# Gathered rows of experts two to eight: loaded in 32 by 32 squares and turned on VectorE, in place of turns on TensorE

## The chip, the core and the metric

The kernel runs on one core of a Trainium2 chip. The core has a matrix engine (TensorE, PE), a vector engine (VectorE, DVE), an activation engine (ScalarE, ACT), a general engine (GpSimd, POOL) and a queue engine (SyncE, SP) that issues transfers; sixteen DMA engines move data between the chip's memory and the on-chip memory of 128 partitions. Each engine works through its own list of instructions in the order written, and they wait for each other by semaphores. The metric is the device time of one execution in microseconds.

## What is computed

A block of a transformer over 16 sequences of 256 tokens with 256 features: cross attention with 16 heads, then a mixture of eight experts of which each token uses two. An expert has room for 640 tokens. All in float32. Cut to what matters here:

```python
x = x + xattn(layernorm(x), ctx)
x_flat = layernorm(x).reshape(4096, 256)
gates = softmax(x_flat @ router_w + router_b)
# per expert: its tokens in order of position, at most 640
buf = zeros((8, 641, 256)).at[expert, slot].add(dispatched)[:, :640]
h = gelu(einsum('ecd,edh->ech', buf, w1) + b1)      # 256 -> 1024
out = einsum('ech,ehd->ecd', h, w2) + b2            # 1024 -> 256
y = einsum('ned,ne->nd', out[expert, slot], gates)
x = x + y
```

## The kernel before

**The table.** While attention runs, GpSimd scatters each token's row into `slot_table` in the chip's memory: 8 x 640 slots, a row of 265 floats (1060 bytes). Columns 0 to 255 are the token's features, column 256 (`ID`) its number, 257 to 264 its gates. The experts gather nothing: expert e reads the 640 rows e x 640 and on.

**Two factors for one.** Every product is taken as three of a reduced float type: a high part (`bufh`, `w1h`, `hidh`), cut on ScalarE or VectorE, and the rest (`bufl`, `w1l`, `hidl`), which VectorE gets by subtraction (`rest_of`, L1072).

Experts are numbered from 0, as in the code: the title's second to eighth are experts 1 to 7.

**An expert.** `up` (L842) has eight chunks j of 128 hidden columns, each with 2 halves of 320 tokens x 2 chunks of features x 3 products = 12 matmuls at L615. ScalarE takes gelu of chunk j (L1044) into one of two `hid` buffers; VectorE splits it into `hidh` (cast, L1328) and `hidl` (L1072) (`split_hid`). `hid` is double buffered, so gelu j waits until chunk j-2 is split, and `up` j waits for gelu j-2. `down` (L862) has five steps of 128 tokens with 8 x 3 = 24 matmuls at L875; in its first step it waits for hidden chunk after hidden chunk. VectorE adds the bias and multiplies with the gate (`weigh`, L1337 and L1338), and GpSimd adds the 128 rows of `y` to the output by an indirect transfer (L591).

**The other factor.** The matmuls of `up` need the tokens' rows with features on the partitions, while a load brings tokens on the partitions. For expert 0 the gather is done by matmuls from the last steps of attention. For experts 1 to 7 `turn_rows` (three calls per expert, of 2, 2 and 1 tiles of 128 tokens) exists on three engines: TensorE turns 128 by 128 tiles through the identity into PSUM (L838), ScalarE copies them to `bufh`, VectorE takes the rest to `bufl`. The calls for expert e+1 stand in `up` of expert e behind chunks 3, 5 and 7 (`TURN_AFTER`); those for expert 1 stand in `down` of expert 0. `up` of an expert waits for its `buf_lo`.

**The loads.** SP issues, for each expert, the rows (`load_rows`, into one of two `rows` buffers, after the y of the expert before the last are written) and behind them both weights (`load_w`, L390 and L391), which all go through one queue in this order. Weights of the next expert are split while `down` runs (`split_w`), pieces alternating with `weigh` on VectorE.

Of the kernel before, what the change touches and what calls it, by code (L numbers as in the profile page):

```python
# [27 lines left out]
P = 128  # L28
B, S, D = 16, 256, 256
# [5 lines left out]
DC = D // P  # L35
NE, HID = 8, 1024
# [14 lines left out]
TURNS = -(-ET // 2)  # L51
TURN_AFTER = (3, 5, 7)
# [125 lines left out]
def build(nc, x, ctxt, wq, wk, wv, wo, bo, rw, rb, w1, b1, w2, b2, out):  # L178
    es = ExitStack()
    with es:  # L180
# [88 lines left out]
        rows = sb(late, "rows", [2, ET, ROW])  # L269
# [56 lines left out]
        def _(sp):  # L326
# [66 lines left out]
            def load_rows(e):  # L393
                if e == 0:
                    sp.dma_start(rows[:, 0, :, D:ROW], table[0:CAP, D:ROW].rearrange("(s p) w -> p s w", p=P))\
                      .then_inc(sem("rows_first"), 16)
                    return
                if e >= 2:
                    sp.wait_ge(sem("y"), ET * (e - 1))
                sp.dma_start(rows[:, e % 2, :, :],  # L400
                             table[e * CAP:(e + 1) * CAP, :].rearrange("(s p) w -> p s w", p=P))\
                  .then_inc(sem(f"rows_in{e % 2}"), 16)
# [195 lines left out]
        def _(pe):  # L598
# [231 lines left out]
            def turn_rows(e, u):  # L830

                rows_ready(pe, e)
                at = TURNS * (e - 1) + u
                pe.wait_ge(sem("buf_lo"), max(2, at + 1))
                for s in range(2 * u, min(2 * u + 2, ET)):
                    for kk in range(DC):
                        col = (s - 2 * u) * D + kk * P
                        mm = pe.transpose(psum[:, at % 2, col:col + P],  # L838
                                          rows[:, e % 2, s, kk * P:(kk + 1) * P], ident[:, :])
                mm.then_inc(sem("turn_rows"), 1)  # L840

            def up(e):  # L842
                r = e % 2
                pe.wait_ge(sem("buf_lo"), 2 + TURNS * e if e else 1)
                pe.wait_ge(sem("wsplit_lo"), WSPLITS * e + WSPLITS // 2)
                for j in range(HC):
# [12 lines left out]
                    if 1 <= e < NE - 1 and j in TURN_AFTER:  # L859
                        turn_rows(e + 1, TURN_AFTER.index(j))  # L860

            def down(e):  # L862
                r = e % 2
                pe.wait_ge(sem("wsplit_lo"), WSPLITS * (e + 1))
                for s in range(ET):
# [12 lines left out]
                    if e == 0 and s < TURNS:  # L878
                        turn_rows(1, s)
# [7 lines left out]
        def _(act):  # L887
# [136 lines left out]
            def turn_rows(e, u):  # L1024
                at, s0, s1 = TURNS * (e - 1) + u, 2 * u, min(2 * u + 2, ET)
                act.wait_ge(sem("turn_rows"), at + 1)
                if e >= 2:
                    act.wait_ge(sem("up"), HC * (e - 1))
                src = psum[:, at % 2, :].rearrange("p (s k c) -> p k s c", k=DC, c=P)
                for kk in range(DC):  # L1030
# [357 lines left out]
```

## Time and profile before

| what | us |
|---|---|
| median of three runs | 1008.44 (1007.81 to 1008.87) |
| the profiled execution, its own time | 1009.7 |
| its span, first to last instruction | 1008.0 |
| TensorE busy | 969.1 (96%) |
| VectorE busy | 780.9 (77%) |
| ScalarE busy | 624.3 (62%) |
| GpSimd busy | 288.5 (29%) |

Attention takes the span up to about 750 us, the eight experts the rest. A busy TensorE isn't TensorE at its peak, since matmuls overlap in the profile; the chain of work that ended last shows how many microseconds a group of them takes of the time. The granted TensorE clock was at its full 1.00 (2.4 GHz) in the stretches of the experts that are read below. A DMA share of 1 means sixteen DMA engines busy; a short window may show more, since a transfer counts where it starts.

### The profile page before, as it was taken

The page shows a single profiled execution, that of the slowest core. Times are in us where ns is not written, and L with a number is a line of the kernel's source. Part 1 is how long each engine was busy: PE and PEld are TensorE (multiplying, and loading weights), DVE is VectorE, ACT ScalarE, POOL GpSimd, SP SyncE. Part 2 cuts the span into 40 slices and gives each one's busy share as a digit, 9 for nine tenths or more (in the row PEclk, how much of TensorE's full clock was granted, in tenths as well). Part 3 has the DMA queues.
Part 4 walks back from the last instruction along what each step waited for, and adds up shares of the span by engine and source line. Part 5 has one row for each costly group of instructions (what it writes and reads, how often), then busy time and mean ns, then how long its engine had stood idle before and what let it go on. Part 6 is the DMA issues. An engine that isn't in the chain of part 4 may idle for free. (4 is left out here: it accounts for less than half of the span.)

```text
span 1008.0 us, 23338 instructions
## 1 busy us (share of the span) xinstructions
PE 969.1 (96%) x8434; PEld 876.0 (87%) x8434; DVE 780.9 (77%) x2093; ACT 624.3 (62%) x1739; POOL 288.5 (29%) x442
## 2 busy tenths in 40 slices
PE   7889999999999999999999999999978999999996
PEld 6778888888888888888888888888768999999995
DVE  6897778878887878878797888877867766777662
ACT  5777776777677767776777677776724333344330
POOL 4542021314132231314123231302253333222233
PEclk9999999999999999999999999999989999999998
DMA  8440101001010101101010101000214543444522
GB/s 240 140 122 2 33 2 33 26 30 54 3 52 15 33 13 33 44 2 44 11 33 6 33 9 33 17 1 16 95 44 154 137 118 75 99 131 127 137 28 27
DMA packets 49057, 56.77 MB, mean 56 GB/s; under 512 B 5948, under 2 KB 44842, under 8 KB 48816
## 3 DMA queue, kind: packets, MB, share of 16 engines
q1 hardware_dynamic: 40112, 46.30, 14.8%
q0 software_dynamic: 8832, 8.98, 5.6%
q8 instruction: 69, 1.13, 0.5%
q14 instruction: 44, 0.36, 0.1%
HBM read 36.01 MB, written 24.20 MB: 60 GB/s over the span
## 5 line engine op out<-in xcount | busy, mean ns | idle before, releaser
L938 ACT ACTIVATE prob<-psum,negmax 128x256 f32<-128x256 f32 x512 | 240.0, 487 | 90.6 <-DVE negmax L1124 89.6
L888 ACT ACTIVATE probt<-psum 128x512 f32<-128x512 f32 x256 | 157.3, 623 | 53.5 <-PE psum L698 52.5
L1124 DVE TENSOR_REDUCE negmax<-psum 128x2 f32<-128x512 f32 x256 | 160.1, 683 | 24.8 <-PE psum L682 24.7
L1135 DVE TENSOR_SCALAR prob<-prob,invtot 128x256 f32<-128x256 f32 x512 | 164.2, 384 | 4.5
L698 PE MATMUL psum<-ident,prob 128*128 128x128 f32 x1024 | 150.5, 273 | 2.4 <-DVE prob L1135 1.6
L1044 ACT ACTIVATE hid<-psum,b1t 128x640 f32<-128x640 f32 x64 | 50.8, 796 | 129.1 <-PE psum L615 124.2
L698 PEld LDWEIGHTS psum<-ident,prob 128*128 128x128 f32 x1024 | 119.7, 140 | 11.7 <-ACT probt L888 2.1
L712 PE MATMUL psum<-probt,v 128*64 128x256 f32 x1024 | 124.6, 385 | 0.0
L550 POOL DMA_INDIRECT slot_table<-row,picki x64 | 66.9, 1045 | 174.6 <-DVE picki L1281 147.5
L591 POOL DMA_INDIRECT out_rows<-y,rowi x40 | 66.8, 1671 | 162.1 <-DVE y L1338 155.1
L938 ACT ACTIVATION_READ_ACCUMULATOR prob<-psum,negmax 128x1 f32 x512 | 112.2, 219 | 0.0
L712 PEld LDWEIGHTS psum<-probt,v 128*64 128x64 f32 x1024 | 67.8, 136 | 36.3 <-issue 0.3
L875 PE MATMUL psum<-w2h,hidh 128*128 128x256 f32 x320 | 92.2, 288 | 1.3 <-DVE hidl L1072 1.3
L485 POOL TENSOR_SCALAR shifted<-ln_mean_var 128x2 f32<-128x2 f32 x32 | 7.3, 229 | 298.7 <-issue 256.4
L875 PE MATMUL psum<-w2l,hidh 128*128 128x256 f32 x320 | 91.0, 285 | 0.0
L875 PE MATMUL psum<-w2h,hidl 128*128 128x256 f32 x320 | 91.0, 284 | 0.0
L682 PE MATMUL psum<-kh,qh 64*128 64x256 f32 x512 | 80.8, 304 | 4.7 <-ACT prob L938 1.7
L615 PE MATMUL psum<-bufh,w1h 128*128 128x320 f32 x256 | 80.4, 314 | 1.4 <-DVE bufl L1072 0.9
L729 PE MATMUL psum<-woh,ah 128*128 128x256 f32 x256 | 75.2, 294 | 6.6 <-DVE kl L1072 5.7
L615 PE MATMUL psum<-xth,wqh 128*128 128x256 f32 x256 | 79.0, 308 | 0.5 <-DVE xtl L1072 0.5
L615 PE MATMUL psum<-bufh,w1l 128*128 128x320 f32 x256 | 79.1, 309 | 0.0
L615 PE MATMUL psum<-bufl,w1h 128*128 128x320 f32 x256 | 79.1, 309 | 0.0
(192 smaller groups left out, 2744.7 us busy)
## 6 DMA issues: line engine op xcount, KB each, us to landing
w1r<-in_w SPq DMA_DIRECT2D x8, 1024.0 KB, 8.2
w2r<-in_w SPq DMA_DIRECT2D x8, 1024.0 KB, 10.4
slot_table<-blank SPq DMA_DIRECT2D x8, 662.5 KB, 9.8
rows<-slot_table SPq DMA_DIRECT2D x7, 662.5 KB, 5.4
xin<-in_x SPq DMA_DIRECT2D x16, 256.0 KB, 2.9
out_rows<-x SPq DMA_DIRECT2D x16, 256.0 KB, 3.2
c<-in_ctxt SPq DMA_DIRECT2D x16, 128.0 KB, 3.1
c<-in_ctxt SPq DMA_DIRECT2D x32, 64.0 KB, 2.8
```

The costliest lines, as they stand in the source:

```text
L550: pool.indirect_dma_start(out=table, out_offset=bass.IndirectOffsetOnAxis(ap=picki[:, b % 3, k, t:t + 1], axis=0), in_=row[:, b % 3, t, :] ...
L591: pool.indirect_dma_start(out=out_rows, out_offset=bass.IndirectOffsetOnAxis(ap=rowi[:, e % 2, s:s + 1], axis=0), in_=y[:, e % 2, s, :], i ...
L615: mm = pe.matmul(dst, lhs, rhs, start=(j == 0), stop=(j == len(terms) - 1))
L682: mm = pe.matmul(psum[:, 2 * cc + h, qb * S:(qb + 1) * S], a[r, m % 2, cc, cols], w[r, m % 2, cc, :], start=(j == 0), stop=(j == len(terms ...
L698: mm = pe.transpose(psum[:, TURN_BANK[u], kb * S + qb * P:kb * S + (qb + 1) * P], prob[:, m % 2, u, qb, kb * P:(kb + 1) * P], ident[:, :])
L712: mm = pe.matmul(dst[h * HD:(h + 1) * HD, cc * S:(cc + 1) * S], v[:, b % 2, kb, cols], probt[:, m % 2, 2 * cc + h, kb, :], start=(kb == 0) ...
L729: mm = pe.matmul(dst[:, 0:D], a[:, b % 2, c, tt], w[:, c, :], start=(c == 0 and j == 0), stop=(c == PAIRS - 1 and j == 2))
L875: mm = pe.matmul(dst, a[:, j, ss], w[:, j, :], start=(j == 0 and m == 0), stop=(j == HC - 1 and m == 2))
L888: copy = lambda dst, src, **kw: act.activation(dst, src, ACT.Copy, **kw)
L938: last = act.activation(prob[:, m % 2, u, qb, :], psum[:, u, qb * S:(qb + 1) * S], ACT.Exp, bias=negmax[:, m % 2, u, qb:qb + 1], accum_out ...
L1124: dve.tensor_reduce(negmax[:, m % 2, u, :], psum[:, u, :].rearrange("p (q s) -> p q s", q=ST), AX.X, ALU.max, negate=True).then_inc(sem("m ...
L1135: last = dve.tensor_scalar(prob[:, m % 2, u, qb, :], prob[:, m % 2, u, qb, :], invtot[:, m % 2, u, qb:qb + 1], None, ALU.mult)
```

## The change

The table, its scatter, and the matmuls of `up` and `down` stay. What changes is how the rows of experts 1 to 7 become `bufh` and `bufl`:

- **Loads.** `rows` keeps only the 9 columns of number and gates. The 256 feature columns come into a new tile `blocks` by eight loads per expert. The load for feature chunk k and group g of 32 features puts, on partition g x 32 + i, row c x 32 + i for all c from 0 to 19, 32 floats of each: squares of 32 tokens by 32 features. Each of these loads is 32 x 20 runs of 128 bytes. They wait for `turned` of the expert before.
- **Turns.** VectorE transposes each 32 by 32 square in place (`square_rows`): one instruction of 128 x 640 for each feature chunk, from `blocks` to `turned`.
- **Splits.** ScalarE copies `turned` to `bufh` (`head_rows`) and VectorE subtracts (`rest_rows`), 128 x 640 each, two per expert in place of six.
- **Places.** In `up` of expert e: the turns behind the split of chunks 1 and 2, heads behind gelu 3 and 4, rests behind chunks 5 and 6. For expert 1 they stand in `down` of expert 0. TensorE has no part in it any more.

```diff
-TURNS = -(-ET // 2)
-TURN_AFTER = (3, 5, 7)
+SQ = 32
+GROUPS = P // SQ
+SQUARE_AFTER = (1, 2)
+HEAD_AFTER = (3, 4)
+REST_AFTER = (5, 6)
...
-        rows = sb(late, "rows", [2, ET, ROW])
+        blocks = sb(late, "blocks", [DC, CAP // SQ, SQ])
+        turned = sb(late, "turned", [DC, CAP])
+        rows = sb(late, "rows", [2, ET, ROW - D])
...
                 if e >= 2:
                     sp.wait_ge(sem("y"), ET * (e - 1))
                 sp.dma_start(rows[:, e % 2, :, :],
-                             table[e * CAP:(e + 1) * CAP, :].rearrange("(s p) w -> p s w", p=P))\
-                  .then_inc(sem(f"rows_in{e % 2}"), 16)
+                             table[e * CAP:(e + 1) * CAP, D:ROW].rearrange("(s p) w -> p s w", p=P))\
+                  .then_inc(sem(done), 16)
+                if e == 0:
+                    return
+                if e >= 2:
+                    sp.wait_ge(sem("turned"), DC * (e - 1))
+                squares = table[e * CAP:(e + 1) * CAP, 0:D].rearrange("(c i) (k g j) -> k g i c j", i=SQ, k=DC, g=GROUPS)
+                for k in range(DC):
+                    for g in range(GROUPS):
+                        sp.dma_start(blocks[g * SQ:(g + 1) * SQ, k, :, :], squares[k, g])\
+                          .then_inc(sem(f"blocks_in{k}"), 16)
...
-                pe.wait_ge(sem("buf_lo"), 2 + TURNS * e if e else 1)
+                pe.wait_ge(sem("buf_lo"), 2 + DC * e if e else 1)
...
-                    if 1 <= e < NE - 1 and j in TURN_AFTER:
-                        turn_rows(e + 1, TURN_AFTER.index(j))
...
-            def turn_rows(e, u):
...
+            def head_rows(e, k):
+                act.wait_ge(sem("turned"), DC * (e - 1) + k + 1)
                 if e >= 2:
                     act.wait_ge(sem("up"), HC * (e - 1))
...
+                copy(bufh[:, e % 2, k, :], turned[:, k, :]).then_inc(sem("buf_hi"), 1)
...
                     for piece in range(WSPLITS):
                         split_w(e + 1, piece)
-                        if e == 0 and piece < TURNS:
-                            turn_rows(1, piece)
+                        if e == 0 and 1 <= piece <= DC:
+                            head_rows(1, piece - 1)
...
+            def square_rows(e, k):
+
+                dve.wait_ge(sem(f"blocks_in{k}"), 16 * GROUPS * e)
+                if e >= 2:
+                    dve.wait_ge(sem("buf_lo"), 2 + DC * (e - 1))
+                dve.transpose(turned[:, k, :], blocks[:, k, :, :].rearrange("p c j -> p (c j)"))\
+                   .then_inc(sem("turned"), 1)
+
+            def rest_rows(e, k):
+                dve.wait_ge(sem("buf_hi"), 2 + DC * (e - 1) + k + 1)
+                rest_of(bufl[:, e % 2, k, :], turned[:, k, :], bufh[:, e % 2, k, :]).then_inc(sem("buf_lo"), 1)
...
                     weigh(e, s)
-                    if e == 0 and s < TURNS:
-                        turn_rows(1, s)
+                    if e == 0 and s == 1:
+                        for k in range(DC):
+                            square_rows(1, k)
+                    if e == 0 and 2 <= s < 2 + DC:
+                        rest_rows(1, s - 2)
```

SP's queue around the loads for one expert, before: rows, then the two weights.

```order
L400 DMA rows<-slot_table 128x5x265
L390 DMA w1r<-in_w 128x2x1024
L391 DMA w2r<-in_w 128x8x256
L400 DMA rows<-slot_table 128x5x265
L390 DMA w1r<-in_w 128x2x1024
```

And after (the line numbers are those of the changed kernel):

```order
L404 DMA rows<-slot_table 128x5x9
L414 DMA blocks<-slot_table 32x20x32 x8
L395 DMA w1r<-in_w 128x2x1024
L396 DMA w2r<-in_w 128x8x256
L404 DMA rows<-slot_table 128x5x9
```

Eight loads stand between the small rows and the weights.

VectorE's order in `up` of an expert, before (a cast and a subtraction per chunk, pairs of rests between):

```order
L1328 CAST hidh<-hid 128x640
L1072 TENSOR_TENSOR hidl<-hid,hidh 128x640
L1072 TENSOR_TENSOR bufl<-psum,bufh 128x256 x2
L1328 CAST hidh<-hid 128x640
L1072 TENSOR_TENSOR hidl<-hid,hidh 128x640
L1328 CAST hidh<-hid 128x640
L1072 TENSOR_TENSOR hidl<-hid,hidh 128x640
L1072 TENSOR_TENSOR bufl<-psum,bufh 128x256 x2
```

This piece runs from chunk 3 to the second pair of rests, behind chunk 5; the third stands behind chunk 7. After, the same engine from chunk 1 on:

```order
L1323 CAST hidh<-hid 128x640
L1064 TENSOR_TENSOR hidl<-hid,hidh 128x640
L1305 STREAM_TRANSPOSE turned<-blocks 128x640
L1323 CAST hidh<-hid 128x640
L1064 TENSOR_TENSOR hidl<-hid,hidh 128x640
L1305 STREAM_TRANSPOSE turned<-blocks 128x640
L1323 CAST hidh<-hid 128x640
L1064 TENSOR_TENSOR hidl<-hid,hidh 128x640
```

and from chunk 5 on:

```order
L1323 CAST hidh<-hid 128x640
L1064 TENSOR_TENSOR hidl<-hid,hidh 128x640
L1064 TENSOR_TENSOR bufl<-turned,bufh 128x640
L1323 CAST hidh<-hid 128x640
L1064 TENSOR_TENSOR hidl<-hid,hidh 128x640
L1064 TENSOR_TENSOR bufl<-turned,bufh 128x640
L1323 CAST hidh<-hid 128x640
L1064 TENSOR_TENSOR hidl<-hid,hidh 128x640
```

Both turns and both rests now stand ahead of the split of chunk 7, the last piece above.

## Rows read from the trace of the kernel before

**Rows 1.** The page, part 1: busy time, share and instructions of each engine.

```profile
PE 969.1 (96%) x8434; PEld 876.0 (87%) x8434; DVE 780.9 (77%) x2093; ACT 624.3 (62%) x1739; POOL 288.5 (29%) x442
```

**Rows 2.** The chain that ended last, experts 0 to 3: start us, us, what.

```profile
792.09 7.04 PE psum L615 x48
...
851.23 7.05 PE psum L615 x48
858.28 0.44 PE psum L838 x4
858.72 3.52 PE psum L615 x24
...
866.21 0.22 PE psum L838 x2
866.42 14.40 PE psum L875 x120
```

**Rows 3.** Timeline of TensorE, expert 3: start us, us, instruction.

```profile
851.07 0.31 PE L615 MATMUL psum<-bufh,w1h 128*128 128x320 f32 x1
```

**Rows 4.** Timeline of VectorE, experts 0 and 3; in brackets the idle time before.

```profile
774.68 0.49 DVE L1328 CAST hidh<-hid 128x640 fp32r<-128x640 f32 x1
...
775.94 0.49 DVE L1328 CAST hidh<-hid 128x640 fp32r<-128x640 f32 x1
...
853.86 0.50 DVE L1328 CAST hidh<-hid 128x640 fp32r<-128x640 f32 x1 [1.78 <-issue]
...
860.42 0.75 DVE L1072 TENSOR_TENSOR bufl<-psum,bufh 128x256 fp32r<-128x256 f32 x2
...
867.60 0.82 DVE L1072 TENSOR_TENSOR hidl<-hid,hidh 128x640 fp32r<-128x640 f32 x1
868.34 0.48 DVE L1072 TENSOR_TENSOR bufl<-psum,bufh 128x128 fp32r<-128x128 f32 x2
```

**Rows 5.** Timeline of ScalarE, the first two gelus of expert 3.

```profile
853.03 0.80 ACT L1044 ACTIVATE hid<-psum,b1t 128x640 f32<-128x640 f32 x1 [11.45 <-PE psum L615]
854.79 0.80 ACT L1044 ACTIVATE hid<-psum,b1t 128x640 f32<-128x640 f32 x1 [0.96 <-PE psum L615]
```

**Rows 6.** Timeline of SP's issues, experts 3 and 4.

```profile
852.11 0.37 SPq L400 DMA_DIRECT2D rows<-slot_table  x1
...
881.70 0.37 SPq L400 DMA_DIRECT2D rows<-slot_table  x1
882.16 0.47 SPq L390 DMA_DIRECT2D w1r<-in_w  x1
882.68 0.47 SPq L391 DMA_DIRECT2D w2r<-in_w  x1
```

**Rows 7.** Landing of the rows of expert 0 (L395); busy time, clock, DMA share, GB/s.

```profile
DMA to landing us min/median/max: 2.0/2.0/2.0
...
767.80:768.00 0.20, 0.20 (x3) 0.20 (x2) 0.20 (x1) 0.20 (x1) 0.20 (x1) 1.00 0.86 46
772.00:773.00 1.00, 1.00 (x9) 1.00 (x8) 0.97 (x2) 0.00 (x0) 0.29 (x1) 1.00 1.05 372
```

**Rows 8.** Last scatter of expert 2 on GpSimd's timeline; windows around the one before.

```profile
852.87 1.57 POOL L591 DMA_INDIRECT out_rows<-y,rowi  x1 [1.34 <-DVE y L1338]
...
852.00:853.25 1.25, 1.25 (x10) 1.25 (x9) 0.08 (x1) 0.22 (x1) 0.38 (x1) 1.00 0.96 105
853.25:853.50 0.25, 0.25 (x4) 0.25 (x3) 0.00 (x0) 0.25 (x1) 0.25 (x1) 1.00 0.12 17
```

**Rows 9.** Weights of expert 1: SP's issue, ScalarE's and VectorE's first piece.

```profile
772.37 0.37 SPq L390 DMA_DIRECT2D w1r<-in_w  x1
...
777.93 1.06 ACT L888 ACTIVATE w1h<-w1r 128x1024 fp32r<-128x1024 f32 x1 [2.28 <-DMA w1r<-in_w]
...
779.10 1.23 DVE L1072 TENSOR_TENSOR w1l<-w1r,w1h 128x1024 fp32r<-128x1024 f32 x1 [1.72 <-ACT w1h L888]
```

**Rows 10.** The page, part 6: KB each, median us from issue to landing.

```profile
w1r<-in_w SPq DMA_DIRECT2D x8, 1024.0 KB, 8.2
```

More of the change, by code:

```diff
@@ L393, in load_rows @@
             def load_rows(e):
[L394 to L397, printed above, removed]
+                done = "rows_first" if e == 0 else f"rows_in{e % 2}"
                 if e >= 2:
@@ L1022, in gathered @@
                 last.then_inc(sem("buf_hi"), 1)
-            def turn_rows(e, u):
-                at, s0, s1 = TURNS * (e - 1) + u, 2 * u, min(2 * u + 2, ET)
-                act.wait_ge(sem("turn_rows"), at + 1)
+            def head_rows(e, k):
+                act.wait_ge(sem("turned"), DC * (e - 1) + k + 1)
                 if e >= 2:
                     act.wait_ge(sem("up"), HC * (e - 1))
-                src = psum[:, at % 2, :].rearrange("p (s k c) -> p k s c", k=DC, c=P)
-                for kk in range(DC):
-                    last = copy(bufh[:, e % 2, kk, s0 * P:s1 * P].rearrange("p (s c) -> p s c", c=P),
-                                src[:, kk, 0:s1 - s0, :])
-                last.then_inc(sem("buf_hi"), 1)
+                copy(bufh[:, e % 2, k, :], turned[:, k, :]).then_inc(sem("buf_hi"), 1)
             for half in range(2):
@@ L1046, in _ @@
                                    bias=b1t[:, e, j:j + 1]).then_inc(sem("gelu"), 1)
-                    if 1 <= e < NE - 1 and j in TURN_AFTER:
-                        turn_rows(e + 1, TURN_AFTER.index(j))
+                    if 1 <= e < NE - 1 and j in HEAD_AFTER:
+                        head_rows(e + 1, HEAD_AFTER.index(j))
                 if e + 1 < NE:
@@ L1306, in gathered @@
                 last.then_inc(sem("buf_lo"), 1)
-            def turn_rows(e, u):
-                at, s0, s1 = TURNS * (e - 1) + u, 2 * u, min(2 * u + 2, ET)
-                dve.wait_ge(sem("buf_hi"), 2 + at + 1)
-                src = psum[:, at % 2, :].rearrange("p (s k c) -> p k s c", k=DC, c=P)
-                for kk in range(DC):
-                    part = lambda a: a[:, e % 2, kk, s0 * P:s1 * P].rearrange("p (s c) -> p s c", c=P)
-                    last = rest_of(part(bufl), src[:, kk, 0:s1 - s0, :], part(bufh))
-                last.then_inc(sem("buf_lo"), 1)
+            def square_rows(e, k):
[7 more added lines that the diff above has]
+                rest_of(bufl[:, e % 2, k, :], turned[:, k, :], bufh[:, e % 2, k, :]).then_inc(sem("buf_lo"), 1)
             def row_numbers(e):
@@ L1320, in row_numbers @@
                     dve.wait_ge(sem("added"), 16 * ET * (e - 1))
-                dve.tensor_copy(rowi[:, e % 2, :], rows[:, e % 2, :, ID]).then_inc(sem("rowi"), 1)
+                dve.tensor_copy(rowi[:, e % 2, :], rows[:, e % 2, :, ID - D]).then_inc(sem("rowi"), 1)
             def split_hid(at):
@@ L1346, in _ @@
                     split_hid(HC * e + j)
-                    if 1 <= e < NE - 1 and j in TURN_AFTER:
-                        turn_rows(e + 1, TURN_AFTER.index(j))
+                    if 1 <= e < NE - 1 and j in SQUARE_AFTER:
+                        square_rows(e + 1, SQUARE_AFTER.index(j))
+                    if 1 <= e < NE - 1 and j in REST_AFTER:
+                        rest_rows(e + 1, REST_AFTER.index(j))
                 row_numbers(e)
```

13 lines of the change are left out of this document (1 added, 12 removed).

## The prediction

> **What bounds the kernel now.** I read the page first: TensorE is busy for 969.1 of 1008.0 us, VectorE for 780.9 [rows 1]. All that the change touches lies in the last quarter, the eight experts. There the chain that ended last is TensorE alone. For expert 3 it reads 7.05 us (four chunks of `up`), 0.44 for four turns, 3.52, 0.44 and 3.52 again, 0.22 for two turns, and 14.40 of `down`: 29.6 us in all and no gap [rows 2]. So an expert costs what TensorE needs, and anything taken off it is a gain until another engine is late. Who would be late is read from the timelines of the same expert. I count from the start of its `up`, 851.07 [rows 3]. A chunk of `up` takes 1.76 us; gelu j ends, and the split of hidden chunk j can begin, at 2.79 + 1.76 j (853.86 for j = 0) [rows 4, 5].
>
> **What TensorE loses.** Ten turns of 128 by 128 per expert take 0.44 + 0.44 + 0.22 = 1.10 us of the chain [rows 2]; 70 in all, 7.7 us for seven experts. This is the most that can be won, 0.8%.
>
> **What VectorE gets.** A split of a hidden chunk holds the engine for 1.27 us when nothing keeps it waiting: cast at 774.68, next cast at 775.94; the subtraction of 640 columns holds it for 0.74 (867.60, next start 868.34) [rows 4]. Before, the rests in `up` were two pairs of 256 and one of 128, 0.75 us for a pair, of which one pair came after chunk 7 [rows 4]. Now there are two turns of 640 columns, after chunks 1 and 2, and two rests of 640, after chunks 5 and 6: all four come ahead of chunk 7. A rest of 640 is the same form as the hidden subtraction, 0.74. A turn by VectorE is not in the trace. Its nearest rows are the cast of 640 (0.49) and that subtraction (0.83 busy, 0.74 held); I take 0.75, since it also passes 640 columns of 4 bytes one by one, and keep 0.5 and 1.5, twice it, as bounds.
>
> Walked through, with the squares always there: chunk 1 is done at 4.55 + 1.27 = 5.82; turn 0 to 6.57; chunk 2 to 7.84; turn 1 to 8.59; chunks 3 and 4 to 11.13; then 0.46 us idle, since gelu 5 allows 11.59; chunk 5 to 12.86; rest 0.74; chunk 6 to 14.88; rest; chunk 7 begins at 15.63 where gelu would have allowed 15.11, and its subtraction ends at 16.98. TensorE now reaches `down` at 14.08 and needs hidden chunk 7 for the 22nd matmul, 21 x 0.12 = 2.52 later (14.40 us over 120 matmuls [rows 2]), at 16.60. Before it had 0.5 us to spare: 866.42 + 2.52 = 868.94 against 867.60 + 0.82 [rows 2, 4]. So there is a stall of 0.4 to 0.45 us per expert that no late transfer causes. The gain is then 0.65 us for each of the six experts turned for within an `up`, not 1.10.
>
> **The squares, on which it hangs.** SP may load the rows of the next expert once the last y of the previous one is written: rows at 852.11, 1.04 after the start, then both weights [rows 6]. Now SP issues the small rows (9 columns), eight square loads, and only then the weights. An issue costs about 0.5 us (881.70, 882.16, 882.68) [rows 6], so the squares are issued at 1.5, 2.0, ... 5.0. A load of 640 runs of 36 bytes landed 2.0 us after its issue [rows 7]; by issue alone the fourth square lands at 5.0 and the eighth at 7.0. VectorE asks for them at 5.82 and 7.84. Because of the 0.46 us idle after chunk 4 they may come at 6.28 and 8.30; every us after that is a us of VectorE, of chunk 7, and so of TensorE. TensorE notices it late, but in full.
>
> Will the transfers keep up with the issues? Each square load is 640 runs of 128 bytes, 320 a DMA engine for all eight. Prices of a run: for 36 bytes, 46 GB/s at a share of 0.86 is 0.86 x 16 x 36 / 46 = 10.8 ns; for the 1060 bytes of a whole row, 372 GB/s at 1.05 is 48 ns [rows 7]. On the line between, 128 bytes cost 10.8 + 92/1024 x 37 = 14 ns. Bounds: 11 (no more than the short one) and 25 (half of the long one). At 14, 320 runs are 4.5 us. They start when the engines have dealt with the scattered rows of y that are still there until 853.25 (share 0.96 up to it, 0.12 behind it [rows 8]), and with the small rows, 640 of which held the engines some 0.65 us at 36 bytes each: at about 2.95. A landing follows its last run by some 0.35. So squares of k = 1 are there at 2.95 + 4.5 + 0.35 = 7.8, in time. But the last scatter of y of the previous expert is issued at 852.87, 1.8 after the start [rows 8], in the midst of them. One such scatter keeps all engines busy for 1.1 us (1.25 us at 0.96 [rows 8]). Before, it competed with rows and weights that nobody awaited for 10 us; now it may stand between the runs of k = 1. With it they land at 8.9. I take this: the lateness is 8.9 - 8.30 = 0.6, the stall 0.45 + 0.6 = 1.05 us, and six experts together gain 6 x 0.05 = 0.3 us.
>
> The Trainium skill ("DMA: Bandwidth & Descriptors", section Why small descriptors are slow) speaks against such loads: a packet costs about 3 cycles beside one for each 32 bytes. As an estimate by that page, 128 bytes cost 7/5 of 36 bytes, 15 ns where the line above gives 14, and the time would be some 2 us longer; no run of the kernel before shows packets of 128 bytes.
>
> **Expert 1, turned for in `down` of expert 0.** Here the squares (issued from about 768) take 4.5 us of the DMA engines where the old rows took 640 x 48 ns / 16 = 1.9, ahead of the weights that are issued at 772.37; ScalarE already waited 2.28 us for these weights, until 777.93, and VectorE 1.72 for ScalarE [rows 9]. They come some 2 us later. In VectorE's order now stand: weight split, y, weight split, y, both turns, weight split, y, rest, weight split, y, rest, y; from 781.1 the second rest ends near 792.7, because the third weight split has to wait for ScalarE, which waits for the first turn before it goes on. `up` of expert 1 waits for that rest; it began at 792.09 before [rows 2]. So the 1.10 us are not won here, and 0.6 is lost (between 1.1 won and 1.5 lost).
>
> **What is hidden.** The weights of the next expert come about 4.5 us later than before (8.2 us after an issue at 1.5 gives 9.7 [rows 10], now near 14); ScalarE wants them after gelu 7, at 15.1, the second half at 17. That just holds; if the squares take 3 us more, it still costs nothing, since the stall then moves gelu 7 too. ScalarE has two copies of 640 instead of six small ones, in an engine that idles 0.96 us before each gelu [rows 5]. Wherever it would stall without this cover, the price is that of the lateness itself.
>
> **The sum.** Profiled execution 1009.7 us (span 1008.0, 1.7 around it), 1.3 above the median 1008.44. Change: -7.7 (turns) + 1.1 (expert 1 keeps nothing of it) + 0.6 (expert 1 late) + 6 x 1.05 (stalls) = +0.3. So 1010.0 for the profiled one and 1008.7, say 1009, for the median.
>
> **The rivals.**
> A, faster: the scatter does not meet the squares, or it does so only behind them, and 128 bytes cost no more than 14 ns. Then the stall is 0.45: -6 x 0.65 + 0.6 = -3.3, 1005.1. If VectorE's turn also costs 0.5 us, the stall is nearly gone: down to 1001. For it: issue and landing alone leave 1.3 us to spare at k = 1. Against it: the scatter's place at 1.8.
> C, slower: the runs are dearer than the line between two prices says, because they are short, start anywhere (a row of the table is 1060 bytes) and fill 32 partitions only. At 20 ns, k = 1 lands at 2.95 + 6.4 + 0.35 + 1.1 = 10.8, the stall is 2.95, the change 6 x 1.85 + 0.6 = +11.7: 1020. At 25 ns 1030. Slower by over 2 us begins at 15 ns with the scatter in between, at 18 without.
> D, slower: a turn on VectorE costs 1.5 us. With forecast landings it adds about 0.75 behind k = 1: +5, 1014.
> E, far slower: the loads are not moved in runs of 128 bytes but in single words. Then 10,240 packets an engine at 10.8 ns are 110 us an expert, against 29.6: beyond 1500 us. The Trainium skill ("VectorE: DVE Perf Modes", The three transpose paths) calls a plain copy that transposes by its strides 19 times slower than the crossbar. Speaking against it: the inner 32 columns stay contiguous on both sides, and the built program has them as 32x20x32.
>
> **How the numbers follow.** The forecast, landing near 8.9 with its own range 1005 to 1013, has 0.40; A (1001 to 1006) 0.30; C (1013 to 1030) 0.24; D 0.05; E 0.01. A measurement of this kernel tells 0.2%, 2 us, from no change. Of the forecast's 0.40 I give 0.05 to faster, 0.24 to the same, 0.11 to slower. So faster 0.35, same 0.24, slower 0.41. The range 1002 to 1023 leaves out the ends of A and C, and E.
>
> **What would show it.** No row of TensorE with `rows`; ten turns gone. In `up`, VectorE's turn near 0.83 us busy, its idle time before the second turn put down to a DMA, 1.1 us or less; the load of `blocks` landing 2.5 to 4 us after issue; TensorE's idle time in `down` before the 22nd matmul, put down to `hidl`, about 1.0 us in each of six experts. An expert's period of 29.5 us would bear the forecast out, 28.9 A, over 30.5 C. I am wrong in kind if TensorE waits for `bufl` or for the weights of experts 2 to 7, or not at all.

## The result, and the profile after

| | before | after |
|---|---|---|
| median, us | 1008.58 (1007.51 to 1009.22, 6 runs) | 1015.06 (1014.34 to 1016.82, 6 runs) |
| ratio | | 1.0068 (95% interval 1.0055 to 1.0081) |
| profiled execution, own time | 1009.7 | 1014.72 |
| its span | 1008.0 | 1012.9 |

The changed kernel is slower by 6.5 us, more than the 2 us that a measurement can tell. The two profiled executions stand 5.0 us apart, because that of before lies above its median and that of after below its own. What follows explains the 4.9 us between the spans; for the rest there are no traces, only a lead at the end of this section.

The page of after, part 1 (answers to [rows 1]):

```profile
PE 966.0 (95%) x8364; PEld 870.5 (86%) x8364; DVE 789.3 (78%) x2079; ACT 621.7 (61%) x1711; POOL 286.7 (28%) x442
```

TensorE has 70 instructions fewer, as the change says, and is busy 3 us less; yet the span is longer. So the question is where TensorE now stands still. The waits of TensorE in the experts (engine, line, waited for: us in total, times, longest):

```profile
PE psum L874 <- DVE hidl L1064: 7.5, 8, 1.1
PE psum L874 <- DVE y L1333: 3.2, 2, 2.6
PE psum L628 <- ACT hid L1036: 0.9, 2, 0.5
PE psum L628 <- DVE bufl L1064: 0.5, 1, 0.5
```

Mostly `down` waits for a hidden chunk (`hidl`), as forecast. Two of these eight waits, 0.64 us each, lie in `down` of expert 0 and are in the kernel before too; the other six, one in each of experts 1 to 6, are new (6.2 us). The two waits for `y` and the one for `bufl` are in expert 0, below. TensorE's timeline at that place in expert 3, whose `up` starts at 855.29 (throughout I take 1.96 us before gelu 0, as 851.07 stands to 853.03 before):

```profile
871.77 0.28 PE L874 MATMUL psum<-w2h,hidl 128*128 128x256 f32 x1
873.09 0.39 PE L874 MATMUL psum<-w2h,hidh 128*128 128x256 f32 x1 [1.04 <-DVE hidl L1064]
```

The idle time in the brackets is less than the stall: matmuls of `down` otherwise start 0.12 us apart, and these two start 1.32 apart, 1.20 later than they could, of which the profile counts only what lies behind the modelled end of the first.

And the chain that ended last, from the last square load of that expert to `down` (start us, us, what), where [rows 2] showed TensorE alone:

```profile
860.10 0.51 SPq L414
...
860.65 3.75 DMA blocks<-slot_table
...
864.43 0.85 DVE turned L1305
...
869.03 0.73 DVE bufl L1064
...
871.03 0.73 DVE bufl L1064
...
872.21 0.84 DVE hidl L1064
...
873.09 10.94 PE psum L874 x89
```

It reads: the eighth issue, 3.75 us until it lands, VectorE from the second turn through five splits and two rests without a pause, and then TensorE. VectorE's timeline (answers to [rows 4]) shows that both turns wait, not only the second:

```profile
861.85 0.84 DVE L1305 STREAM_TRANSPOSE turned<-blocks 128x640 f32<-128x640 f32 x1 [0.66 <-DMA blocks<-slot_table]
862.62 0.45 DVE L1323 CAST hidh<-hid 128x640 fp32r<-128x640 f32 x1
...
864.43 0.85 DVE L1305 STREAM_TRANSPOSE turned<-blocks 128x640 f32<-128x640 f32 x1 [0.50 <-DMA blocks<-slot_table]
865.20 0.45 DVE L1323 CAST hidh<-hid 128x640 fp32r<-128x640 f32 x1
```

A turn holds VectorE for 0.77 us (861.85 to 862.62). In the numbers below "turn 0/turn 1" is the start of the two turns after the start of `up`, and the period is from one `up` to the next. An expert without turns would take 28.49 us: the 29.58 us of [rows 2]'s kind less 1.10, and experiment D shows it six times.

| expert in whose `up` the turns stand | 1 | 2 | 3 | 4 | 5 | 6 |
|---|---|---|---|---|---|---|
| turn 0 | 8.19 | 6.78 | 6.56 | 6.83 | 6.70 | 6.57 |
| turn 1 | 10.35 | 9.36 | 9.14 | 9.41 | 8.92 | 9.14 |
| period | 30.98 | 30.01 | 29.78 | 30.05 | 29.56 | 29.77 |
| stall (period - 28.49) | 2.49 | 1.52 | 1.29 | 1.56 | 1.07 | 1.28 |

The 4.9 us are: +2.7 in these six periods (180.15 against 6 x 29.58), +1.83 in expert 0 (34.63 us from its gelu 0 to that of expert 1, before 32.80), and some +0.45 that begins ahead of the experts (gelu 0 of expert 0 is at 761.63 instead of 761.09) and is partly made good in the last. This last part isn't the change's: in the twelve profiles of this document, all with the same attention, that gelu stands anywhere from 760.04 to 762.79.

Expert 0's part starts in SP's queue (answers to [rows 6] and [rows 9]), then ScalarE's and VectorE's first weight pieces, and expert 1's first gelu:

```profile
768.58 6.90 SPq L414 DMA_DIRECT2D blocks<-slot_table  x8
775.59 0.45 SPq L395 DMA_DIRECT2D w1r<-in_w  x1
```

```profile
780.79 2.00 ACT L885 ACTIVATE w1h<-w1r 128x1024 fp32r<-128x1024 f32 x2 [4.60 <-DMA w1r<-in_w]
...
796.26 0.80 ACT L1036 ACTIVATE hid<-psum,b1t 128x640 f32<-128x640 f32 x1 [6.12 <-PE psum L628]
```

```profile
781.95 1.23 DVE L1064 TENSOR_TENSOR w1l<-w1r,w1h 128x1024 fp32r<-128x1024 f32 x1 [4.04 <-ACT w1h L885]
```

The weights of expert 1 are issued at 775.59 instead of 772.37. ScalarE waits 4.60 us for them instead of 2.28, VectorE 4.04 instead of 1.72. VectorE does the first y of expert 0 behind that split, and TensorE has to stop for it, 2.6 us, since `down` has two halves of PSUM for its steps.

The 32.80 us that this is compared with hold something else. I wrote of the kernel before that TensorE's clock was full in all the stretches read. It wasn't: in `down` of expert 0 its profile has 3.4 us at the lower of the two levels (1.2 GHz, granted share 0.50), which begin just after TensorE had waited twice for a hidden chunk. The kernel after has none there. The windows of before, then of after:

```profile
777.40:780.80 3.40, 3.40 (x16) 3.40 (x17) 1.67 (x3) 2.66 (x4) 0.00 (x0) 0.50 0.72 241
```

```profile
777.80:781.20 3.40, 3.31 (x27) 3.29 (x27) 0.11 (x2) 0.41 (x1) 0.00 (x0) 1.00 1.02 392
```

From 777.35 on, with 99 matmuls and all ten turns to go, TensorE took 14.74 us until 792.09, where 99 x 0.12 + 1.10 = 12.98 would do: about 1.7 us go to the clock. At full clock before, expert 0 is about 3.5 us dearer after the change, not 1.83, and the spans would stand 6.6 us apart, which is what the medians show (6.5). That the unprofiled executions of the kernel before lack this stretch is likely by that, but not shown. Expert 0 also differs by itself: in eight of the changed kernels (after, A, B, D, F, G, H, M) TensorE, VectorE and ScalarE have the same work in it, and it takes from 34.54 to 35.86 us.

### The profile page after: what moved, and what is told of

Same layout as the page of the kernel before. It is cut to its first block and busy times, and to the rows that moved or that the text cites. A ratio compares the mean times of both kernels' runs of the same rounds, so it can differ in the third digit from the quotient of the medians.

```text
span 1012.9 us, 23197 instructions
## 1 busy us (share of the span) xinstructions
PE 966.0 (95%) x8364; PEld 870.5 (86%) x8364; DVE 789.3 (78%) x2079; ACT 621.7 (61%) x1711; POOL 286.7 (28%) x442
```

## The experiments

My theory after the result: the stall is the sum of two causes, VectorE's order (both rests ahead of chunk 7) and the late arrival of the squares; the arrival is late because the runs of 128 bytes need the DMA engines longer than forecast, with a scatter among them; and expert 0 pays for weights queued behind squares. Rivals: the arrival is set by SP's issues (eight at 0.55 us), or the scatter alone makes it late, or the order on VectorE matters little. Each run below stands beside runs of the kernel before on the same chip; its ratio is to those. In the kernel after, the ratio was 1.0068.

### A. The rests behind chunk 7

```diff
-                    if 1 <= e < NE - 1 and j in REST_AFTER:
-                        rest_rows(e + 1, REST_AFTER.index(j))
+                    if 1 <= e < NE - 1 and j == HC - 1:
+                        for k in range(DC):
+                            rest_rows(e + 1, k)
```

> The changed kernel with one move: the two rests of 128x640 on VectorE stand behind the split of hidden chunk 7 instead of behind chunks 5 and 6. Theory (VectorE's chain from the second turn to chunk 7 is too long, and TensorE waits for chunk 7 in the first step of down): the chain gets 1.48 us shorter, the waits for chunk 7 in experts 2 to 6 (1.1 to 1.6 us) all but go, that of expert 1 (2.5) falls to about 1, some 8 us in all: 1007. Rival (only the arrival of the squares counts, and VectorE has room behind it): no change, 1015.

Measured: 1010.0 us (1008.44 to 1012.25, 10 runs), ratio 1.0008 (0.9998 to 1.0017). That is between the 1007 of the theory and the 1015 of its rival: about 0.6% comes back for two rests, 1.48 us of VectorE, that no longer stand ahead of chunk 7. The turns wait as before (6.68 and 9.32 in expert 3), and the periods are 30.90, 29.41, 28.79, 29.14, 28.66, 28.67. With turn 1 at 9.15 and 9.20 (experts 5 and 6) only 0.17 is left of the stall, as much as M below has with no late square at all; with 11.45 and 9.94 (experts 1 and 2) there is more, 2.2 and 0.7. So lateness up to about 9.2 is absorbed, and what is beyond it is paid in full. It is paid at another place than forecast: TensorE no longer waits for a hidden chunk in `down` of these experts, but in `up` for gelus (0.90 and 0.82 us in expert 1), which wait for late splits. The gain was larger than the order's own 0.45 x 6, because it also swallows lateness.

### B. Only the squares of k = 0 are loaded, experts 2 to 7

```diff
-                for k in range(DC):
+                for k in range(DC if e == 1 else 1):
...
-                dve.transpose(turned[:, k, :], blocks[:, k, :, :].rearrange("p c j -> p (c j)"))\
+                dve.transpose(turned[:, k, :], blocks[:, k if e == 1 else 0, :, :].rearrange("p c j -> p (c j)"))\
```

> The changed kernel, but for experts 2 to 7 only the four square loads of feature chunk 0 are made, and both turns read them; the half of the rows with features 128 to 255 is left out, so the output is not the reference's. VectorE's work and order are unchanged. Theory (the late arrival of the second four loads adds to the stall): turn 1 no longer waits, the stall falls from 1.1 to 1.6 us to 0.5 to 0.7 in experts 2 to 6 and by more in expert 1: about 5 us less, 1010. Rival (VectorE's longer order alone makes the stall): 1015. Rival (the loads cost nothing but their issue on SP): the same 1010 with the turn's wait gone, so this one does not tell issue from transfer.

Measured: 1014.72 us (1012.51 to 1015.36, 4 runs), ratio 1.0057 (1.0041 to 1.0074). A miss, and the most useful one: half the bytes and half the issues (2.18 us in place of 4.90) bring almost nothing (the profiled execution, 1012.51, is the lowest of the four). Turn 1 reads what the loads of k = 0 brought and has no wait of its own. VectorE's timeline, expert 3 of this kernel, whose `up` starts at 853.28:

```profile
860.10 0.84 DVE L1306 STREAM_TRANSPOSE turned<-blocks 128x640 f32<-128x640 f32 x1 [0.92 <-DMA blocks<-slot_table]
```

Turn 0 is at 6.82, as late as in the kernel after (6.56). Turn 1 then follows it directly, 2.0 later, at 8.82. My sum had put the scatter behind the squares of k = 0 and let turn 0 be in time; it is turn 0 that the scatter meets first. Periods were 30.41, 29.35, 29.46, 30.36, 29.63, 29.35; in expert 4, where turn 0 is at 7.72, the period is longer than with the full load (30.05).

### C. The weights of expert 1 ahead of its squares

```diff
-            load_rows(1)
+            load_rows(1, (0,))
             load_w(1)
+            load_rows(1, (1,))
```

(Part 0 of `load_rows` is the small rows, part 1 the squares.)

> The changed kernel, but for expert 1 SP issues both weights ahead of the eight square loads. Theory (in down of expert 0, 1.8 us are lost because the weights of expert 1 are issued at 775.6 instead of 772.4 and come 3 us later): ScalarE has w1r near 777.9 again; the squares then come near 784, about when VectorE asks for them; up of expert 1 starts 1 to 2 us earlier, 1013.5. Rival (the loss there comes from VectorE's and ScalarE's new order of turns, heads and rests): no change, 1015.

Measured: 1015.37 us (1014.53 to 1017.35, 4 runs), ratio 1.0068 (1.0049 to 1.0087). No change in the time, yet expert 0 has its 1.1 us: 33.56 from gelu 0 to gelu 0 instead of 34.63 and below all eight profiles named above; ScalarE waits 1.8 us for w1 instead of 4.6. The six periods took it back: 181.57 against 180.15, with turn 1 anywhere from 8.81 to 10.39. This run showed that arrival differs by over 0.5 us from expert to expert and from kernel to kernel though nothing near those loads was changed, and that one repair can't be read from the total while the other stall stands.

### D. All row work of experts 2 to 7 in `down` of the expert before

```diff
-                    if 1 <= e < NE - 1 and j in SQUARE_AFTER:
-                        square_rows(e + 1, SQUARE_AFTER.index(j))
-                    if 1 <= e < NE - 1 and j in REST_AFTER:
-                        rest_rows(e + 1, REST_AFTER.index(j))
...
+                    if 1 <= e < NE - 1 and 1 <= s < 1 + DC:
+                        square_rows(e + 1, s - 1)
+                    if 1 <= e < NE - 1 and s == 3:
+                        for k in range(DC):
+                            rest_rows(e + 1, k)
```

The heads go behind the weight splits on ScalarE.

> The changed kernel with all row work of experts 2 to 7 moved from up to down of the expert before: turns behind the y of steps 1 and 2, both rests behind that of step 3, the heads behind the weight splits. The loads stay. Theory: down leaves VectorE some 6 us idle, the squares are there 8 us before they are asked for, TensorE waits for nothing: period 28.5 us for six experts, -9.3 us: 1006. Rival (the loads of 128-byte runs themselves hold up weights, scatters or the split of hidden chunks): periods stay above 29, 1009 or more.

Measured: 1005.57 us (1004.89 to 1006.00, 6 runs), ratio 0.9963 (0.9951 to 0.9976): faster than before. The chain from `up` of expert 2 on:

```profile
822.84 14.08 PE psum L628 x96
836.92 14.41 PE psum L874 x120
851.33 14.08 PE psum L628 x96
865.41 14.41 PE psum L874 x120
```

TensorE alone, 28.49 us an expert six times over; the turns wait for nothing at 20.8 and 23.7. This is [rows 2] without its turns, and the 1.10 us of the forecast's first term is all there: 29.58 - 28.49 = 1.09.

### F. The fifth scatter of experts 0 to 6 left out

```diff
-                for s in range(ET):
+                for s in range(ET if e == NE - 1 else ET - 1):
```

(and the counts that wait for it; the fifth tile of y is not added for these experts.)

> The changed kernel without the scatter of the fifth tile of y (tokens 512 to 639) of experts 0 to 6, which is left out, so those rows of the output lack a part. It is issued 1.8 us after up starts, amid the square loads. Theory (it holds the DMA engines for about 1 us while the squares of chunk 0, or of chunk 1, are on their way, and makes the first turn start at 6.6 to 6.8 us and the second at 9.1 to 9.4 after the start of up): turn 0 at 6.0, turn 1 at 8.3, the stall per expert 1.3 -> 0.5, expert 1 gains 1 more: 1015 -> 1009. Rival (runs of 128 bytes are slow by themselves, or their start is what is late): turns where they are, 1015.

Measured: 1011.63 us (1010.84 to 1013.24, 5 runs), ratio 1.0030 (1.0017 to 1.0044). Turn 0 comes in time in experts 2, 3, 5 and 6 (5.92, 5.82, 5.87, 5.90), where it came at 6.56 to 6.78. So the scatter is what made turn 0 late in these. In expert 4 it is at 6.80 all the same; SP's eight issues took 5.38 us there instead of 4.38. But turn 1 hardly gains: 8.50, 8.92, 9.57, 9.04, 8.66 in experts 2 to 6, a mean of 8.94 against 9.19. I had expected 8.3. The windows of this kernel in expert 3, `up` from 852.80, tell why (window, its length, busy us and count of PE, PEld, DVE, ACT, POOL, clock, DMA share, GB/s):

```profile
855.75:860.80 5.05, 5.05 (x37) 5.05 (x36) 4.44 (x7) 2.35 (x4) 0.00 (x0) 1.00 0.88 134
...
855.80:856.80 1.00, 1.00 (x9) 1.00 (x8) 0.97 (x2) 0.28 (x1) 0.00 (x0) 1.00 0.73 105
...
859.80:860.30 0.50, 0.50 (x6) 0.50 (x5) 0.47 (x2) 0.26 (x1) 0.00 (x0) 1.00 0.42 66
```

The busy time is 5.05 x 0.88 = 4.44 us for 320 runs an engine, 13.9 ns for one. (The bytes in the window are some 3% more than the squares', so this is a little high; the trace's own packets of 128 bytes there take 13.7 ns on average.) But they are not packed: at the beginning the share is 0.73, near the end 0.42, and the second turn starts at 861.72, 8.92 after `up`. By these packets the stream begins 2.75 us after `up` and its last one ends at 8.35, so it is 5.6 us long; the landing follows 0.54 later.

### G. Each square load with half its runs, experts 2 to 7

```diff
-                        sp.dma_start(blocks[g * SQ:(g + 1) * SQ, k, :, :], squares[k, g])\
+                        c = CAP // SQ if e == 1 else CAP // SQ // 2
+                        sp.dma_start(blocks[g * SQ:(g + 1) * SQ, k, 0:c, :], squares[k, g][:, 0:c, :])\
```

> The changed kernel; for experts 2 to 7 each of the eight square loads brings only rows 0 to 319 (10 squares of 20 for each group; the rest of the tile keeps what it had), so the output is not the reference's. Same eight issues on SP, half the runs. Theory (transfer of the runs, 0.7 to 0.9 us per load, sets the arrival, not the issue at 0.55): turn 0 at 6.0 or earlier, turn 1 no longer waits for a DMA (8.0 or earlier), 5 to 6 us less: 1009. Rival (SP's issues set it): turns stay where they are, 1015. Rival (the scatter in between holds them whatever their number): turn 0 stays at 6.6 or later, turn 1 is better, 1013.

Measured: 1009.92 us (1008.49 to 1011.67, 10 runs), ratio 1.0012 (1.0003 to 1.0021). Eight issues as before (4.15 to 4.17 us in most experts), half the runs, and over 5 us come back. Turn 1 follows turn 0 by 2.0 in all six; three of the periods are 28.96 or 28.97. So it isn't SP's pace that makes turn 1 late, but the runs in the transfers. They act on SP as well: in the kernel after, one or two of the eight issues took about 1 us in each of experts 2 to 6, and the eighth went out at 5.4 to 6.2 after `up`; here it went out at 5.1 to 5.2 (expert 4: 6.2). How much of the lateness goes through these held-up issues, and how much through the engines alone, no run separates. Turn 0 still comes at 5.90 to 7.30.

### H. The squares issued as soon as their tile is free, 20 us earlier

```diff
-            load_rows(2)
+            load_rows(2, (1,))
+            load_rows(2, (0,))
...
-                    load_rows(e + 1)
+                    load_rows(e + 1, (1,))
+                    load_rows(e + 1, (0,))
```

(Part 1 is the squares again; they no longer wait for y, only for `turned`, and the small rows stay where they were.) All computing stays where it was. The squares are issued 8.7 us after the start of the `up` before, and the weights no longer stand behind them.

> The changed kernel, all instructions of the compute engines in their places; SP issues the squares of an expert as soon as the tile is free again, before it waits for y: some 20 us before they are turned, while the small rows stay where they are. Theory (two terms make the stall, the squares' arrival and VectorE's order): the arrival is gone, the order remains: split of chunk 7 ends 0.52 us later than in an expert without row work, period 28.49 + 0.52 = 29.0 in all six experts (now 29.6 to 31.0), 6 us less: 1009. Rival (arrival alone): period 28.5, 1006. Rival (order alone): 1015.

Measured: 1008.08 us (1006.76 to 1009.74, 10 runs), ratio 0.9998 (0.9989 to 1.0008). VectorE's timeline, expert 3 of this kernel (`up` from 851.55):

```profile
857.37 0.84 DVE L1308 STREAM_TRANSPOSE turned<-blocks 128x640 f32<-128x640 f32 x1
...
859.36 0.84 DVE L1308 STREAM_TRANSPOSE turned<-blocks 128x640 f32<-128x640 f32 x1
...
866.41 0.82 DVE L1067 TENSOR_TENSOR bufl<-turned,bufh 128x640 fp32r<-128x640 f32 x1
867.14 0.48 DVE L1326 CAST hidh<-hid 128x640 fp32r<-128x640 f32 x1
```

Both turns at 5.82 and 7.81, the split of chunk 7 from 15.59: the forecast's walk gave 5.82, 7.84 and 15.63. Every period is 28.97. So the order costs 28.97 - 28.49 = 0.48 an expert, and arrival the rest, on average 30.02 - 28.97 = 1.05. The two causes are shown apart.

### M. Both: squares early and rests behind chunk 7

Against H:

```diff
-                    if 1 <= e < NE - 1 and j in REST_AFTER:
-                        rest_rows(e + 1, REST_AFTER.index(j))
+                    if 1 <= e < NE - 1 and j == HC - 1:
+                        for k in range(DC):
+                            rest_rows(e + 1, k)
```

> The changed kernel with the squares issued as soon as their tile is free, and the two rests behind the split of chunk 7. Turns stay in up behind chunks 1 and 2. Theory (the stall is the sum of the squares' arrival and of VectorE's order ahead of chunk 7): both gone, period 28.49 in all six experts, 3 us less than with early squares alone: 1005. Rival (the two turns alone, 1.5 us between chunks 1 and 3, still push chunk 7): period above 28.6.

Measured: 1005.98 us (1005.31 to 1007.51, 10 runs), ratio 0.9983 (0.9974 to 0.9992). Chunk 7 is ready at 16.46, as without any row work, but the periods are 28.65, not 28.49. The timelines of VectorE and of TensorE in `down` of expert 3:

```profile
869.58 0.41 DVE L1335 TENSOR_TENSOR y<-psum,b_all 128x256 f32<-128x256 f32 x1
870.03 0.35 DVE L1336 TENSOR_SCALAR y<-y,rows 128x256 f32<-128x256 f32 x1
```

```profile
870.25 0.28 PE L877 MATMUL psum<-w2h,hidl 128*128 128x256 f32 x1
870.43 0.39 PE L877 MATMUL psum<-w2h,hidh 128*128 128x256 f32 x1
870.66 0.28 PE L877 MATMUL psum<-w2l,hidh 128*128 128x256 f32 x1
```

The rests push the first y back to 870.38, and the third step of `down`, which takes over the PSUM half of the first, begins at 870.43: matmuls that elsewhere start 0.12 us apart are 0.18 and 0.23 apart here, 0.17 us in all. It fits the 0.16; it is read from these rows and wasn't tried apart.

### E. D, and the weights of expert 1 first

The edits of D and C together.

> Row work of experts 2 to 7 in down of the expert before, and for expert 1 the weights issued ahead of the squares. Theory: periods 28.49 as with the first alone, and the time from the first gelu of expert 0 to that of expert 1 falls from 34.8 to 33.6 us, as where only the weights were put first: 1005.6 - 1.2 = 1004.4, faster than both kernels. Rival (the weights' place does nothing): 1005.6.

Measured: 1004.60 us (1003.77 to 1005.61, 5 runs), ratio 0.9961 (0.9948 to 0.9975); D had 0.9963, so the total doesn't tell them apart. In the trace, gelu 0 to gelu 0 of expert 0 is 34.18 instead of D's 34.81, half of the 1.2 us that the theory asked for. Now the squares come late for the turns that stand behind y step 1:

```profile
786.03 0.84 DVE L1308 STREAM_TRANSPOSE turned<-blocks 128x640 f32<-128x640 f32 x1 [2.29 <-DMA blocks<-slot_table]
```

and TensorE waits for y behind them, once for 2.3 us.

### K. E, and in expert 0 the turns one y later, all row copies behind the weights

Against E:

```diff
-                        if e == 0 and 1 <= piece <= DC:
-                            head_rows(1, piece - 1)
-                    if 1 <= e < NE - 1:
+                    if e < NE - 1:
...
-                    if e == 0 and s == 1:
+                    if e == 0 and s == 2:
...
-                    if 1 <= e < NE - 1 and s == 3:
+                    if e < NE - 1 and s == 3:
...
-                    if e == 0 and 2 <= s < 2 + DC:
-                        rest_rows(1, s - 2)
```

> All row work in down, weights of expert 1 ahead of its squares, and in down of expert 0 both turns stand behind the y of step 2 (not step 1), the heads behind all four weight splits, both rests behind the y of step 3. Theory (with the squares behind the weights, VectorE stood 2.3 us before the second turn with the y of step 2 behind it, and TensorE waited 2.3 us for that y): the wait goes, up of expert 1 starts some 1.9 us earlier, 1004.6 - 1.9 = 1002.7. Rival (what is saved there comes back as a wait of up for the rests): 1004.6.

Measured: 1001.38 us (1000.79 to 1002.43, 5 runs), ratio 0.9933 (0.9919 to 0.9947), faster than both kernels. Expert 0 takes 31.38 us from gelu 0 to gelu 0, 2.8 less than in E where 1.9 were expected. That is 1.42 less than in the profile before the change, but 1.7 us of that profile are the lower clock, which K doesn't have there: at like clock expert 0 is still some 0.3 us dearer than before. TensorE's waits in the experts:

```profile
PE psum L630 <- DVE bufl L1065: 1.5, 2, 0.9
PE psum L876 <- DVE hidl L1065: 1.3, 2, 0.6
PE psum L630 <- ACT hid L1038: 0.5, 1, 0.5
```

The wait for y is gone, and of the waits for hidden chunks (7.5 in the kernel after) only the 1.3 us of expert 0 are left that the kernel before has too. A part of what was saved does come back as waits of `up` for the rests, of which E had none. By the ratio 6.8 us are won (5.3 to 8.2) of the 7.7 that TensorE was relieved of.

## Why the prediction was right or wrong

Forecast 1009, range 1002 to 1023; measured 1015.06. The range holds it and slower had the largest of the three chances, but the likeliest time is 6 us off, and the change of +0.3 stands against +4.9 in the profiles. That the range holds it says little: it spans 21 us and covers rivals with other mechanisms, and 1015 lies beyond the forecast's own 1005 to 1013. The kind of wait and its place were right (TensorE for `hidl`, 0.8 to 1.1 us in each of six experts; VectorE for a DMA); the terms that were off are the landing of the squares and expert 0.

- **TensorE's turns, -7.7 us: right.** D gives 1.09 us an expert; in K 6.5 us are won in the six periods.
- **VectorE's turn, 0.75 us taken: right.** It is 0.84 busy, 0.75 to 0.77 held. Rival D (1.5 us) is out.
- **VectorE's order, 0.45 us a stall: right.** H measures 0.48, with each time of the walk within 0.04.
- **That a late turn 1 costs every us behind 8.30: right.** 0.45 + (turn 1 - 8.30) gives 1.34 on average for experts 2 to 6, where 1.34 was measured, and 2.50 for expert 1 (2.49).
- **The arrival, "With it they land at 8.9": mis-sized.** Turn 1 started at 9.39 on average over the six. The price of a run was right, 13.7 to 13.9 ns (F), and so, nearly, was the start: 2.75 where 2.95 was forecast. (The small rows were put at 0.65 us; 40 an engine at the forecast's own 10.8 ns are 0.43.) Two other parts were off, in opposite directions. First, "At 14, 320 runs are 4.5 us" took the engines to be packed; without that scatter the landing was at 8.9 instead of 7.8 (F, expert 3), as the stream took 5.6 us, 1.1 more. Second, the scatter, put in at its full 1.1 us behind the squares of k = 0, added only 0.25 to turn 1 (9.19 against 8.94). It was luck that these two nearly cancel; with the first error alone the forecast would have been 10.0. Why the scatter cost so little is seen in the windows of the kernel after, ahead of it, around it and behind it:

```profile
858.30:859.30 1.00, 1.00 (x9) 1.00 (x8) 0.97 (x2) 0.29 (x1) 0.36 (x1) 1.00 0.68 89
...
860.30:862.30 2.00, 2.00 (x15) 2.00 (x15) 1.31 (x3) 0.80 (x1) 0.00 (x0) 1.00 1.31 202
...
861.79:862.29 0.50, 0.50 (x5) 0.50 (x4) 0.44 (x1) 0.00 (x0) 0.00 (x0) 1.00 1.34 208
```

The stream had room at 0.68 before the scatter came. Behind it, when the trace has no packet of the scatter left (the last window), the squares that had queued up moved at 208 GB/s, 16 x 128 / 208 = 9.8 ns a run and engine, faster than 13.9: the packets' times add up to 1.34 of the sixteen engines, so the time of a packet isn't its engine's alone. For the same reason neither 4.4 nor 4.5 us is the least that 320 runs need.

- **"Now it may stand between the runs of k = 1": the place was wrong.** It met those of k = 0, and turn 0, assumed in time, came at 6.6 to 6.8 where 6.28 is allowed (B, F). In experts 2 to 6 this didn't add to the stall, since turn 1 was later still; it is why B gained so little.
- **All six experts alike: wrong.** `up` of expert 1 met two scatters, because y of expert 0 was late (first rows below, GpSimd; that `up` starts at 794.30). Its turn 1 came at 10.35, a stall of 2.49, so that 1.4 of the 2.7 us (30.98 - 29.58) lie in this one expert. What the chain shows directly (second rows) is SP: its seventh issue took 2.86 us, so that the eighth went out at 7.56 after `up` instead of 5.4 to 6.2, and landed 2.76 behind it, where expert 3 took 3.75. With one scatter less (F) the longest issue there took 1.78 us, with half the runs (G) 0.92; so both bear on it, but why an issue is held isn't shown.

```profile
794.21 1.53 POOL L604 DMA_INDIRECT out_rows<-y,rowi  x1 [0.39 <-issue]
796.05 1.62 POOL L604 DMA_INDIRECT out_rows<-y,rowi  x1 [0.30 <-issue]
```

```profile
798.96 2.86 SPq L414
...
801.87 2.76 DMA blocks<-slot_table
...
804.65 0.84 DVE turned L1305
```

- **Expert 0, "0.6 is lost": mis-sized, 1.83, and some 3.5 at like clock.** I had counted the data ahead of the weights (4.5 - 1.9 us) and left the weights' issue at 772.37. But SP itself was held up: eight issues took 6.90 us in place of 8 x 0.55 = 4.4, and the weights stood behind them. And I had followed the chain through the second rest only (792.7; it ended at 794.16, 793.35 + 0.81), not through the first y, whose delay of 2.6 us stops TensorE. And the 792.09 that it started from has 1.7 us of the lower clock in it.
- **What was called hidden: right.** The only wait for w1 in the experts is that of expert 1; ScalarE's two copies delay nobody.
- **The rivals.** A needed the squares in time, as H made them; even H gives 1008, not 1005, since expert 0 costs more than forecast there too (35.1 us from gelu 0 to gelu 0). The time lies in the range of C, "the runs are dearer" (1013 to 1030), but the mean stall of 1.53 is nearer to the forecast's 1.05 than to C's 2.95, and C's mechanism, the price of a run, isn't what was seen; the stream was thin. E is out; the page, part 6 (KB each, median us from issue to landing), has the squares landing soon:

```profile
blocks<-slot_table SPq DMA_DIRECT2D x56, 80.0 KB, 3.1
```

The Trainium skill ("VectorE: DVE Perf Modes", The three transpose paths) has a plain copy that transposes by strides, where the innermost stride of the target is large, at 19 times the crossbar's time; this load, with 32 columns contiguous on both sides, isn't such a copy, and no run here has one. The estimate of 15 ns, worked out from the cycles of the page "DMA: Bandwidth & Descriptors" of the Trainium skill (Why small descriptors are slow) and the row of 36 bytes, lies close to the 13.9 that F shows.

What stays open: why the stream is uneven and single issues are held (one load after another at 0.55 us with 40 runs an engine, 32 target partitions each, rows that start at multiples of 1060 bytes: no run took these apart), why turn 1 of equal experts differs by up to 0.5 us, and whether the 1.6 us by which the medians stand further apart than the profiles are indeed the lower clock in expert 0 of the profile before. The mean granted clock bears on the unprofiled executions too: it is 0.988 to 0.991 in the six of the kernel after and 0.988 to 0.994 in those of the kernel before beside runs A to D.

## What to carry to other kernels

Work taken from the engine that sets the time is a gain only as far as its new engine has idle time at that very place; here `up` had 0.5 us to spare on VectorE and `down` had enough for all of it, and the same work there, in expert 0 too, gave -0.7% in place of +0.7%. Ask of every load in small pieces where the consumer stands with respect to its landing, leave it a microsecond or two beyond what runs times price gives, and issue it as soon as its tile is free. When one load becomes eight, look at what stands behind them in the issuing queue, and follow the delay through every reader, not only through the one that the change is about.

## What the runs showed of the hardware

- A stretch of 5120 runs of 128 bytes in eight loads takes 13.9 ns a run in busy time, but 5.6 us from its first packet to its last where 320 x 13.9 ns are 4.4 (F, expert 3). A backlog of them passed at 9.8 ns a run and engine, at a DMA share of 1.34 (kernel after, expert 3).
- SP's issue isn't of constant price. The squares' issues and VectorE's turns in the kernel after (duration in ns, min/median/max; first and last start):

```profile
L414 SPq DMA_DIRECT2D blocks<-slot_table x56: 504/516/2863, 768.6 to 950.6; - x56
...
L1305 DVE STREAM_TRANSPOSE turned<-blocks x14: 796/845/847, 786.0 to 953.8; 128x640 f32<-128x640 f32 x14
```

One issue in a row of eight took up to 2.86 us where the others take 0.52, and eight behind both weights took 9.76 us in all (E). Whoever is behind it in the queue is issued later by that much.
- A scatter of 128 rows that alone holds the sixteen engines for 1.1 us delayed a thin stream beside it by 0.25 us at its end (turn 1), and by 0.6 at its middle (turn 0, 6.69 against 6.06 in F, mean of experts 2 to 6).
- TensorE's granted clock was 0.50 for 3.4 us in `down` of expert 0 of the kernel before, which cost about 1.7 us; in D a stretch like it stands ahead of TensorE's wait for y, which is 1.27 us there and 2.7 in M, where the clock is full: expert 0 takes 34.81 us in D and 34.79 in M.
